# Cross-attention's row of score maxima: built by VectorE from 32x32 turns and partition-quarter copies instead of by TensorE transposes

## The reference, cut to what matters

```python
q = _split_heads(x @ Wq)      # 16 heads of 32
k = _split_heads(y @ Wk)
v = _split_heads(y @ Wv)
attn = jnp.einsum('bhid,bhjd->bhij', q, k) * SCALE
attn = jax.nn.softmax(attn, axis=-1)
out = jnp.einsum('bhij,bhjd->bhid', attn, v)
```

## Time and profile before

| what | value |
|---|---|
| median of three runs | 1843.1 us |
| the profiled execution | 1845.33 us, of which 1843.4 us are the span from first to last instruction |
| mean granted TensorE clock | 0.997 |
| busy: VectorE, ScalarE, GpSimd | 1133.7, 842.2 and 904.1 us |
| cross-attention in the span | from about 60 to 1520 us |

### The profile page before, as it was taken

How to read it: one execution, slowest core, us unless ns; L and a number is a source line. 1 busy time by engine, 2 the same in 40 slices (tenths; PEclk the granted TensorE clock), 3 DMA queues, 4 the chain that set the end, 5 groups by cost and what they waited for, 6 DMA issues and landing times. The chain is left out here.

```text
span 1843.4 us, 65602 instructions
## 1 busy us (share of the span) xinstructions
PE 1821.4 (99%) x28988; PEld 1588.2 (86%) x28988; DVE 1133.7 (62%) x1366; ACT 842.2 (46%) x1046; POOL 904.1 (49%) x830
## 2 busy tenths in 40 slices
PE   8999999999999999999999999999999999999998
PEld 7979898989898989898989898988898877787887
DVE  6654848484747474757575666656575767574265
ACT  4634545454545454545444444544454533334332
POOL 0334727383838383828273737464645573434111
PEclk9999999999999999999999999999999999999999
DMA  6210202020202020202020202020111122023110
GB/s 240 119 53 2 83 3 82 3 82 4 82 4 82 4 82 3 82 4 82 3 82 4 82 3 82 9 77 19 66 40 45 55 100 90 23 92 103 47 58 23
DMA packets 43358, 101.18 MB, mean 55 GB/s; under 512 B 19121, under 2 KB 20657, under 8 KB 42961
## 3 DMA queue, kind: packets, MB, share of 16 engines
q1 hardware_dynamic: 43088, 96.88, 14.9%
HBM read 86.48 MB, written 8.29 MB: 51 GB/s over the span
## 5 line engine op out<-in xcount | busy, mean ns | idle before, releaser
L553 POOL TENSOR_TENSOR fold<-fold,prob 128x256 f32<-128x256 f32 (+1 forms) x704 | 723.1, 1027 | 55.2
L111 PE MATMUL ring<-y_parts,w_keep 128*128 128x402 f32 (+1 forms) x3072 | 607.6, 351 | 1.6 <-PEq L189 1.4
L111 PEld LDWEIGHTS ring<-y_parts,w_keep 128*128 128x128 f32 x3072 | 551.4, 188 | 16.1 <-issue 2.8
L111 PE MATMUL ring<-wv_s,y_parts 128*128 128x512 f32 x2304 | 552.2, 396 | 0.0
L111 PEld LDWEIGHTS ring<-wv_s,y_parts 128*128 128x128 f32 x2304 | 427.8, 188 | 95.4
L547 POOL TENSOR_TENSOR fold<-prob 128x256 f32<-128x256 f32 x64 | 68.2, 1066 | 656.1 <-ACT prob L608 656.1
L573 ACT ACTIVATE k_sb<-ring 128x402 f32<-128x402 f32 (+1 forms) x256 | 129.5, 506 | 362.6 <-PE ring L111 362.6
L753 DVE TENSOR_TENSOR prob<-prob,peak_rows 128x1024 f32<-128x1024 f32 (+1 forms) x192 | 275.2, 1486 | 13.4 <-ACT peak_rows L604 13.4
L598 ACT ACTIVATE prob<-s_ps 128x1536 f32<-128x1536 f32 (+1 forms) x128 | 200.0, 1562 | 132.2 <-PE s_ps L903 132.2
L608 ACT ACTIVATE prob<-prob 128x1024 f32<-128x1024 f32 (+1 forms) x192 | 207.5, 1123 | 4.7 <-DVE prob L753 2.9
L730 DVE TENSOR_TENSOR fold<-prob 128x512 f32<-128x512 f32 x64 | 50.9, 796 | 212.5 <-ACT prob L598 212.5
(11 more groups left out here) (212 smaller groups left out, 1580.3 us busy)
## 6 DMA issues: line engine op xcount, KB each, us to landing
y_raw<-yT SPq DMA_DIRECT2D x48, 804.0 KB, 6.5
y_raw<-yT SPq DMA_DIRECT2D x16, 792.0 KB, 9.2
f_raw<-w_ffn SPq DMA_DIRECT2D x22, 512.0 KB, 3.5
v_sb<-y_left SPq DMA_DIRECT2D x1, 2304.0 KB, 11.3
v_sb<-v_left SPq DMA_DIRECT2D x16, 130.0 KB
p_x<-x SPq DMA_DIRECT2D x4, 512.0 KB, 6.6
q_scratch<-p_x SPq DMA_DIRECT2D x8, 256.0 KB, 2.0
q_sb<-q_scratch SPq DMA_DIRECT2D x16, 128.0 KB, 8.8
```

Source lines behind the costliest of these rows:

```text
L111: mm = pe.matmul(out, left(a, c), right(b, c), start=(c == 0 and n == 0), stop=(c == DC - 1 and n == 2))
L553: pool.tensor_tensor(acc[0:m], acc[0:m], prob[0:m, i, t, :], ALU.add).then_inc(sum_step, 1)
```

## The change

Steps 2 to 4 and the copy of step 5 go. `row_of_peaks` does them on VectorE alone: a 32x32-blockwise transpose of `fold`, a maximum within each block (128x8), three copies that bring partition quarters 1 to 3 beside quarter 0 (each 32x8), a maximum over the four (32x8), three copies of that back to quarters 1 to 3, and a second blockwise transpose, reading each value 32 times, that writes `peak_rows`. These are ten instructions on one queue; waits on `row_step` stand between all but the copies of a group. VectorE's order is changed around it, the TensorE order loses the turns and the waits that came with the shared bank, and GpSimd waits for `fold_read` (the first transpose) instead of `turn_ok`. In the first batch `left_high` and `left_low` come one block earlier.

```diff
-        peak = sb("peak", [P, 2])
+        quarters = sb("quarters", [P, P // SQ, HQ // SQ])
+        peak = sb("peak", [P, HQ // SQ])
...
-                pool.wait_ge(turn_ok, NBLK * b + i + 1)
+                pool.wait_ge(fold_read, NBLK * b + i + 1)
...
-            def peak_row(b, i):
-                act.wait_ge(spread_ok, NBLK * b + i + 1)
-                act.activation(peak_rows[:], spread, ACT.Copy).then_inc(row_ok, 1)
...
-                    if not past and i == 2:
+                    if not past and i == 1:
                         for j in range(LEFT_SLOTS):
                             left_high(j)
...
-            def peaks(b, i):
+            def row_of_peaks(b, i):
                 block = NBLK * b + i
-                dve.wait_ge(turn_ok, block + 1)
-                dve.tensor_reduce(peak[:], turned.rearrange("p (k j) -> p k j", k=2), AX.X,
-                                  ALU.max).then_inc(peak_ok, 1)
+                step = ROW_N * block
+                first = slice(0, SQ)
+                others = [(k, slice(k * SQ, (k + 1) * SQ)) for k in range(1, P // SQ)]
+                dve.wait_ge(tree, TREE_N * (block + 1))
+                dve.transpose(peak_rows[:], fold[:, i, :]).then_inc(fold_read, 1)
+                dve.wait_ge(fold_read, block + 1)
+                dve.tensor_reduce(quarters[:, 0, :], peak_rows[:].rearrange("p (j q) -> p j q", q=SQ), AX.X,
+                                  ALU.max).then_inc(row_step, 1)
+                dve.wait_ge(row_step, step + 1)
+                for k, rows in others:
+                    dve.tensor_copy(quarters[first, k, :], quarters[rows, 0, :]).then_inc(row_step, 1)
+                dve.wait_ge(row_step, step + 4)
+                dve.tensor_reduce(peak[first, :], quarters[first].rearrange("p k j -> p j k"), AX.X,
+                                  ALU.max).then_inc(row_step, 1)
+                dve.wait_ge(row_step, step + 5)
+                for k, rows in others:
+                    dve.tensor_copy(peak[rows, :], peak[first, :]).then_inc(row_step, 1)
+                dve.wait_ge(row_step, step + 8)
+                dve.transpose(peak_rows[:].rearrange("p (j q) -> p j q", q=SQ),
+                              peak[:].unsqueeze(2).broadcast_to((P, HQ // SQ, SQ))).then_inc(row_step, 1)
...
                 largest(b, 0, 0)
-                if past:
-                    output(b - 1, 1)
                 largest(b, 0, 1)
                 for i in (1, 2):
-                    peaks(b, i - 1)
+                    row_of_peaks(b, i - 1)
+                    subtract(b, i - 1)
                     largest(b, i, 0)
-                    if not past and i == 2:
+                    if past:
+                        output(b - 1, i)
+                    elif i == 1:
                         for j in range(LEFT_SLOTS):
                             left_low(j)
-                    subtract(b, i - 1)
                     largest(b, i, 1)
-                    if past:
-                        output(b - 1, i + 1)
+                if past:
+                    output(b - 1, 3)
+                row_of_peaks(b, 2)
+                subtract(b, 2)
...
                 value(b, 0)
-                peaks(b, 2)
                 largest(b, 3, 0)
-                subtract(b, 2)
                 value(b, 2)
                 largest(b, 3, 1)
+                row_of_peaks(b, 3)
                 value(b, 4)
+                subtract(b, 3)
                 if more:
                     low(b + 1, 0)
-                peaks(b, 3)
                 value(b, 6)
-                subtract(b, 3)
                 value(b, 8)
...
             def batch(b, past):
-                keys(b, 0, 0)
-                keys(b, 0, 1)
-                if past:
-                    small_rows(b - 1, 3)
-                    weigh(b - 1, 0)
-                keys(b, 0, 2)
-                keys(b, 0, 3)
-                keys(b, 1, 0)
-                scores(b, 0, 0)
-                keys(b, 1, 1)
-                scores(b, 0, 1)
-                keys(b, 1, 2)
-                if past:
-                    small_output(b - 1, 0)
-                    weigh(b - 1, 1)
-                keys(b, 1, 3)
-                for i in (2, 3):
+                for i in range(NBLK):
                     keys(b, i, 0)
+                    if i:
+                        scores(b, i - 1, 0)
+                    keys(b, i, 1)
+                    if i:
+                        scores(b, i - 1, 1)
+                        keys(b, i, 2)
                     if past:
-                        small_output(b - 1, i - 1)
-                    else:
-                        small_rows(b, i - 3)
-                    turn(b, i - 2)
-                    scores(b, i - 1, 0)
-                    keys(b, i, 1)
-                    spread_peaks(b, i - 2)
-                    scores(b, i - 1, 1)
-                    keys(b, i, 2)
-                    if past:
-                        small_rows(b, i - 2)
+                        small_read(b - 1, i - 1)
                         weigh(b - 1, i)
+                    if i == 0:
+                        keys(b, i, 2)
                     keys(b, i, 3)
```

More of the change, by code:

```diff
@@ L47 @@
 TREE_N = 7
+SQ = 32
+ROW_N = 9
 PIECES = ((0, 4), (4, 8), (8, JT))
@@ L420, in cross_attention @@
         small_ps = ctx.enter_context(nc.psum_tensor("small_ps", [P, 512], F32))
-        turned, spread = small_ps[:, 0:HQ], small_ps[:, HQ:2 * HQ]
         full, act_out, dve_out = sem("ring_full"), sem("ring_act_out"), sem("ring_dve_out")
         q_in, s_full, s_out = sem("q_in"), sem("s_full"), sem("s_out")
-        tree, turn_ok, peak_ok = sem("tree"), sem("turn_ok"), sem("peak_ok")
-        spread_ok, row_ok, sub_ok, exp_ok = sem("spread_ok"), sem("row_ok"), sem("sub_ok"), sem("exp_ok")
+        tree, fold_read, row_step = sem("tree"), sem("fold_read"), sem("row_step")
+        sub_ok, exp_ok = sem("sub_ok"), sem("exp_ok")
         sum_step, pv_ok, rec_ok, o_out, o_stored = (sem("sum_step"), sem("pv_ok"), sem("rec_ok"), sem("o_out"),
@@ L632, in keys_phase @@
                     key(b, i, 1)
-                    if i >= 2:
-                        peak_row(b, i - 2)
                     score(b, i - 1, 1)
@@ L655, in values_phase @@
                 value(b, 1)
-                peak_row(b, 2)
                 score(b, 3, 1)
@@ L667, in values_phase @@
                 value(b, 5)
-                peak_row(b, 3)
                 if more:
@@ L742, in largest @@
                                   ALU.max).then_inc(tree, 1)
-            def peaks(b, i):
+            def row_of_peaks(b, i):
                 block = NBLK * b + i
-                dve.wait_ge(turn_ok, block + 1)
-                dve.tensor_reduce(peak[:], turned.rearrange("p (k j) -> p k j", k=2), AX.X,
-                                  ALU.max).then_inc(peak_ok, 1)
+                step = ROW_N * block
[18 more added lines that the diff above has]
+                              peak[:].unsqueeze(2).broadcast_to((P, HQ // SQ, SQ))).then_inc(row_step, 1)
             def subtract(b, i):
-                dve.wait_ge(row_ok, NBLK * b + i + 1)
+                dve.wait_ge(row_step, ROW_N * (NBLK * b + i + 1))
                 for n in range(len(PIECES)):
@@ L905, in scores, with small_read @@
                 mm.then_inc(s_full, 1)
[L907 to L924, removed]
+            def small_read(b, i):
                 reached(pe, o_out, NBLK * b + i + 1)
@@ L984, in batch @@
                 scores(b, 3, 0)
[L985 to L988, removed]
+                if not past:
                     left_emptied(LT - 1)
                 values(b, 1)
[L991 to L995, removed]
-                scores(b, 3, 1)
[L997 to L1003, removed]
+                scores(b, 3, 1)
+                for t in range(2, VT):
                     values(b, t)
@@ L1020, in _ @@
             out_ahead(0)
-            small_rows(B - 1, 3)
             weigh(B - 1, 0, last_bank(0))
```

## The result

The changed kernel takes 1885.1 us (median; 1882.7 to 1887.0), the kernel before 1842.7 us in the same set of runs: ratio 1.023, 95% interval 1.021 to 1.025. It is slower by 42 us where 27 were forecast. The profiled execution took 1887.0 us, its span is 1885.0 us.

What follows compares the result with a forecast made beforehand. TensorE, busy 99% of the span, was taken as the bound. From 1845.3 us, 28.2 gained against 55 of new waits for VectorE made +27; less 2.2 to the median, 1870 us, slower; range 1815 to 1925.

Steps and rivals of the forecast that it cites:

- the likeliest case: One or two of the four follower copies wait out a GpSimd addition: R of 3.55 to 4.9, 1847 to 1908 us; chance 0.36.
- TensorE's gain: Turns and spreading transposes leave TensorE: 0.22 us a pair, eight pairs a batch, 16 batches, 28.2 us gained.
- The row alone: One row of maxima on VectorE without GpSimd interference: three 256-element instructions, seven tiny ones and five waits, 2.6 us.
- The row beside GpSimd: Rows of blocks 1 to 3: each group's first copy waits 0.4 us, one of four followers 0.65 more, 4.05 us.
- all four followers waiting: Upper end of the much slower rival, three or four followers waiting: R 5.35 to 6.0, 1928 to 1958 us; chance 0.16.
- The first due time: `weigh(b-1, 3)` needs `output(b-1, 2)`, ready at 645.4 + R; TensorE comes at 648.3, so it waits R - 2.9.
- R: Time of one row on VectorE beside GpSimd, taken as 4.05 us; bounds 2.2 and 6.0, break-even at 3.45.
- The later due times: `values(b, 3)`, `values(b, 7)` and `values(b, 9)` need `value(b, 0)`, `value(b, 4)` and `value(b, 6)`; the last adds 1.2 us of wait.
- 3R - 8.5: TensorE's new waits per batch over all four due times: 3.7 us at R = 4.05, 55 us in fifteen batches.
- The row of block 2: Its row, like those of blocks 1 and 3, runs beside GpSimd additions and takes R, 4.05 us.
- The first batch: Its left-over part moves one block earlier; it may gain the 2.0 us TensorE waits there or lose as much; taken as 0.
- Rival A: GpSimd does not noticeably hold up the small copies: R of 2.2 to 2.85, all 28.2 us gained, 1815 us; chance 0.22.

## Why the prediction was right

It forecast 1870 us and slower, and 1885 came, inside the range of 1815 to 1925 and of the likeliest case's 1847 to 1908. By its steps:

- **TensorE's gain, 28.2 us.** The run with the row left out gives 26, and 1.65 instead of 1.76 us a batch. The busy time, some 50 us, would have been nearly double. Right.
- **The row alone, 2.6 us.** 2.77. The turns, which no row had shown, take 0.445 us where 0.42 was taken, and followers come 0.19 us apart.
- **The row beside GpSimd, 4.05 us.** 4.33. The prediction took a leader that waits in each group and one of four followers that loses a round. The trace has one of the two followers in each group, two of four, but each wait is shorter: in the row shown 0.31 and 0.44 us, in the whole trace 0.30 to 0.54. The Trainium skill's rule (SBUF - State Buffer, Who interferes with whom) that copies within SBUF can be blocked by GpSimd and reductions are not is borne out for 32x8 elements: copies up to 705 ns, one-element maxima never over 156. The Trainium skill's other rule (VectorE: DVE Perf Modes, Two Vector instructions with no wait between them), that a change of partition quarter holds an instruction until the earlier ones have ended, agrees with 0.19 against 0.07 us. But the outcome that the prediction tied to it, all four followers waiting, did not come: a held follower of 0.16 us still fits in between two additions once in two.
- **The first due time.** Forecast R - 2.9 = 1.4 us with the measured R; it was 2.28. The walk put the output's end at 645.4 + R, which is 666.6 us on the clock of the batch shown, and it was 667.4: the two maxima at 664.33 took 2.3 us where 1.9 were taken, and the rest is spread.
- **The later due times.** The sum of 3R - 8.5 was too high: it gives 4.5 us for R = 4.33, where batches without a fall of the clock are 2.9 to 3.1 us longer than those of the run without the row. The term that was too large is the walk from `value(b, 0)` to `value(b, 4)`. Two maxima, a copy, five maxima and a copy were taken as 8.5 us beside the row; they take 7.2, from 681.84 to 693.38 us less the row of 4.35. So `value(b, 4)` is ready in time, and behind the first wait only 0.3 us at `value(b, 6)` is left (VectorE, then TensorE):

```profile
681.16 0.68 DVE L703 COPY v_sb<-ring 128x512 f32<-128x512 f32 x1
...
692.73 0.65 DVE L703 COPY v_sb<-ring 128x512 f32<-128x512 f32 x1
```
```profile
679.96 19.73 PE L113 MATMUL ring<-wv_s,y_parts 128*128 128x512 f32 x84
...
699.96 8.61 PE L113 MATMUL ring<-wv_s,y_parts 128*128 128x512 f32 x36 [0.28 <-DVE v_sb L703]
```

- **The row of block 2.** It was forecast beside GpSimd, and takes 4.5 us in the four batches with output to give and no fall of the clock, but 2.77 us in just the 11 batches with a fall. There TensorE's key product comes late, ScalarE copies it out before it takes the last exponentials, and GpSimd runs out of tiles for 1.50 us while the copies pass (first the batch without a fall, then one with):

```profile
673.71 1.50 DVE L752 COPY quarters<-quarters 32x8 f32<-32x8 f32 x3
```
```profile
580.79 0.50 ACT L575 ACTIVATE k_sb<-ring 128x396 f32<-128x396 f32 x1 [5.51 <-PE ring L113]
...
581.26 0.55 DVE L752 COPY quarters<-quarters 32x8 f32<-32x8 f32 x3
...
582.61 2.41 POOL L555 TENSOR_TENSOR fold<-fold,prob 128x256 f32<-128x256 f32 x2 [1.50 <-ACT prob L606]
```

- **What was not foreseen.** The clock: 15 us. The first batch, where 0 was taken from bounds of 2 either way: the step that moved row and subtraction of block 2 ahead of the left-over tiles was not costed. It is 10 us against the run with the left-over tiles first, and about 7 us against the kernel before, whose first batch has a wait of 2.0 us and a fall of the clock of its own. Last, the end of cross-attention: there TensorE pauses for 3.0 us, and a fall of the clock stands behind it, some 4 us together; every run of the changed kernel has such a pause of 2.3 to 3.0 us, also the one with the row left out, and the kernel before has none over 0.32. No run here shows what brings it about.

In sum, from the traces: 26 us gained (16 batches at 1.65), 15 x 2.9 = 44 us of waits in the loop, 15, 7 and 4 us of the three terms above, which makes +44; +42 were measured, and the forecast was -28 + 55 = +27. Terms of 26 us were missing and the waits of the loop had been put 11 us too high. That 1885 still lies in the likeliest case's range is in part luck; the direction and its cause, copies held up by GpSimd that make VectorE miss due times, are not.

Rival A was wrong by its condition, that small copies pass unhindered, and right in its price: the kernels where that holds take 1816 to 1834 us.

## What to carry to other kernels

When work moves from a saturated engine to one with spare time, the load is not the price: write down, for each thing that the full engine takes from the other, when it is due and what stands before it in the queue. Here an engine 62% busy before the change was late by 2 us at an instruction behind the row, and moving that one instruction alone only moved the wait; the 15 us that it saved were the clock's. Choose small instructions by what they share: a copy between SBUF tiles was held up by GpSimd in 37 rows of 64, and the same move written as a maximum over one element did not.

## What the runs showed of the hardware

- A wait of 2.28 us on TensorE, between stretches of full work, was followed by a stretch at half clock in 11 of 14 cases, about 1.4 us lost each, and in 11 of 14 again in the run with the left-over tiles first; one of 2.04 us in the first batch of the kernel before was followed by one too; one of 1.58 us and all those of up to 1.4 us in the loops of these runs were followed by none. The pause of 2.3 to 3.0 us at the end of cross-attention was followed by one in six of the nine changed runs, so the length alone does not settle it. In the loop the clock thus adds more than half to the price of the one wait, and nothing to the smaller ones.
- A VectorE copy of 32x8 elements takes 0.16 us alone and up to 0.70 us beside GpSimd additions; the same as a maximum over one element takes 0.15 us, and never over 0.156 us in 384 instructions, 288 of them with a GpSimd instruction beside them.
- Copies of 32x8 elements that follow one another and change partition quarter come 0.19 us apart, those that stay in one quarter 0.07.
- Where the clock fell, TensorE's late product reached GpSimd by way of ScalarE's queue: GpSimd stood idle for 1.50 us, and six VectorE copies that had taken 1.50 and 1.37 us a group of three took 0.55.
- A blockwise 32x32 turn of 128x256 fp32 elements takes 0.445 us, its broadcast form the same.
